# Dynamic filters on one core: Newton step through the PSUM bank of the gelu's input, and all nine products summed by TensorE

## What is computed

```python
h = x
for _ in range(STEPS):                      # STEPS = 5
    t = gelu(einsum('oc,bchw->bohw', W1, h) + b1)
    k = (einsum('oc,bchw->bohw', W2, t) + b2).reshape(B, C, 9, H, W)
    k = k / (norm(k, axis=2) + EPS)         # EPS = 1e-6
    y = sum(patches3x3(h) * k, axis=2)
    h = h + alpha * y
```

## Time and profile before

| | |
|---|---|
| Median of 3 runs | 20135.72 us (20120.86 to 20145.39) |
| Profiled execution | 20080.48 us, span 20078.7 us |
| TensorE / VectorE / ScalarE / GpSimd busy over the span | 62% / 52% / 28% / 47% |
| Mean granted TensorE clock | 0.736 |
| First work of the filter stage | about 15575 us from the start |

### The profile page before, as it was taken

One profiled execution on the slowest core, in us unless ns is written; L12 is line 12 of the kernel. 1 busy time (PEld: TensorE's weight loads), 2 busy tenths in 40 slices (PEclk: granted clock), 3 DMA queues, 4 the chain that ended last, 5 costly groups with the idle time before them and its releaser, 6 DMA issues. The chain is left out here.

```text
span 20078.7 us, 217701 instructions
## 1 busy us (share of the span) xinstructions
PE 12353.6 (62%) x73490; PEld 6114.7 (30%) x73490; DVE 10535.6 (52%) x14652; ACT 5526.4 (28%) x7765; POOL 9453.1 (47%) x8026
## 2 busy tenths in 40 slices
PE   5553699999999202333333333333358899999998
PEld 2551366666666101111111111111112333333332
DVE  4557544444444333443443444344422788888887
ACT  1114333333333000000000000000010666666666
POOL 0113100000000106886887788688800787878787
PEclk9999856656666556666666666666679999999999
DMA  4104222222222494335334433533342112121201
GB/s 94 33 21 102 55 38 36 37 38 36 36 37 38 135 195 111 95 95 131 95 95 107 120 95 95 131 96 95 95 86 58 33 22 42 21 42 22 42 19 30
DMA packets 1399772, 1408.47 MB, mean 70 GB/s; under 512 B 771709, under 2 KB 1116045, under 8 KB 1383565
## 3 DMA queue, kind: packets, MB, share of 16 engines
q1 hardware_dynamic: 1106892, 742.84, 18.5%
q0 software_dynamic: 221184, 604.27, 10.4%
q10 hardware_dynamic: 70976, 50.83, 0.8%
HBM read 1036.74 MB, written 276.84 MB: 65 GB/s over the span
## 5 line engine op out<-in xcount | busy, mean ns | idle before, releaser
L1359 POOL DMA_INDIRECT dc_g<-corners,dc_idx x4608 | 5253.7, 1140 | 1326.0 <-issue 1260.9
L1954 POOL TENSOR_TENSOR df_sq<-df_sq 128x512 f32<-128x512 f32 x1920 | 2713.0, 1427 | 1866.6 <-ACT df_sq L1902 1839.5
L1432 PE MATMUL dc_ps<-ident,dc_s 128*128 128x128 f32 x2560 | 674.0, 428 | 4296.9 <-DVE dc_s L1523 4294.8
L1079 POOL TENSOR_TENSOR nz_vp<-nz_vp,nz_den 128x2048 f32<-128x2048 f32 x16 | 105.8, 6610 | 4814.7 <-DMA nz_den<-den_d 4814.7
L1515 DVE TENSOR_TENSOR dc_g<-dc_g,dc_wt 128x2304 f32<-128x2304 f32 x512 | 1308.6, 2556 | 2001.0 <-DMA dc_g<-corners,dc_idx 2000.9
L1902 ACT ACTIVATE df_sq<-df_pk,vecs 128x512 f32<-128x512 f32 x2880 | 1921.1, 685 | 1326.0 <-DVE df_pr L2056 1309.2
L2056 DVE SCALAR_TENSOR_TENSOR df_pr<-df_pk,vecs,df_h 128x512 f32<-128x512 f32 x2880 | 2047.6, 741 | 407.1 <-PE df_pk L1840 264.5
L1432 PEld LDWEIGHTS dc_ps<-ident,dc_s 128*128 128x128 f32 x2560 | 472.0, 218 | 4480.6 <-DVE dc_s L1523 3352.1
L1392 ACT ACTIVATE dc_st<-dc_ps 128x512 f32<-128x512 f32 x640 | 327.0, 607 | 4934.2 <-PE dc_ps L1432 4934.2
L1840 PE MATMUL df_pk<-df_t,df_wp 64*128 64x512 f32 x3840 | 1389.8, 642 | 364.7 <-ACT df_sq L1902 302.1
L916 DVE TENSOR_REDUCE at_mx<-at_pt 128x4 f32<-128x512 f32 x1024 | 707.8, 691 | 1605.4 <-PE at_pt L779 1605.4
(11 more groups left out here) (271 smaller groups left out, 19428.1 us busy)
## 6 DMA issues: line engine op xcount, KB each, us to landing
df_h<-df_h SPq DMA_DIRECT2D x160, 512.0 KB, 7.1
dc_g<-corners,dc_idx POOLq DMA_INDIRECT x4608, 2.8
corners<-dc_xt SPq DMA_DIRECT2D x16, 4160.0 KB, 41.5
dc_xp<-x SPq DMA_DIRECT2D x8, 4096.0 KB, 40.8
cv_xp<-x SPq DMA_DIRECT2D x8, 4096.0 KB, 50.0
y<-sp_p SPq DMA_DIRECT2D x128, 192.0 KB, 2.8
y<-sp_p SPq DMA_DIRECT2D x64, 384.0 KB, 4.3
at_a<-y SPq DMA_DIRECT2D x64, 384.0 KB
```

Source lines behind the costliest of these rows:

```text
L1359: nc.gpsimd.indirect_dma_start(gt[:, r, k, :, :].rearrange("p a c -> p (a c)"), None, image, bass.IndirectOffsetOnAxis(ap=idx[:, s, r, k:k ...
L1432: i = nc.tensor.transpose(ps[:, j, 128 * r:128 * r + 128], sm[:, r % 2, 128 * j:128 * j + 128], env.ident[:, :])
L1954: nc.gpsimd.tensor_tensor(a, a, sq[:, (KK * n + other) % RING, :], ALU.add).then_inc(nadded, 1)
```

## The change

- GpSimd no longer adds products 6 and 7. TensorE adds products 6, 7 and 8 through the identity, six half-width matmuls in place of two; VectorE's join of y is a copy from PSUM.
- The check writes to the bank `df_p` (p1), which held the gelu's input, instead of to SBUF in place. Refinement reads and writes that bank, and update reads it.
- Check, refinement, update and residual of chunk n - 6 (LAG = 6) stand behind products 0, 1, 2 and 3 of chunk n, in every chunk. The scaling of chunk n - 5 stands behind GpSimd's fourth addition.
- The hidden matmul of chunk n also waits for the update of chunk n - 7; the check waits for the gelu of its own chunk.
- Stores and loads of the raw input go by chunk, with a semaphore for each of four buffers, and the order on SyncE in the last step is new.

```diff
-    BANKS, RING = 5, 15
+    BANKS, RING, LAG = 5, 15, 6
...
+        def wait_update(eng, n):
+            b, step, g = GROUPS[n // CH]
+            if step < STEPS - 1:
+                eng.wait_ge(moved, CH * updates(b, step + 1, g) - CH + n % CH + 1)
+            else:
+                eng.wait_ge(stepout, CH * (b * GR + g) + n % CH + 1)
...
+            def load_raw(o):
+                for src, p in piece(x3, o):
+                    sp.dma_start(rows(ro[p, o % CH, :]), src).then_inc(raw_in[o % CH], 16)
+
+            def store(o):
+                sp.wait_ge(o_out, o + 1)
+                for dst, p in piece(out, o):
+                    sp.dma_start(dst, rows(yo[p, o % CH, :])).then_inc(stored[o % CH], 16)
...
+                for i in range(CH):
+                    o = CH * (b * GR + g) + i
+                    store(o)
+                    if o + CH < CH * B * GR:
+                        load_raw(o + CH)
+                    if i == 1 and g and b + 1 < B:
+                        sp.wait_ge(normed, (b + 1) * GR + g)
+                        copy(g - 1)
+                if b + 1 < B:
                     sp.wait_ge(stepout, CH * (b * GR + g + 1))
-                    if b + 1 < B:
-                        load(b + 1, g)
-                    sp.wait_ge(o_out, CH * (b * GR + g + 1))
...
+                    load(b + 1, g)
...
                 if n:
                     pe.wait_ge(active, n)
+                if n >= LAG + 1:
+                    wait_update(pe, n - LAG - 1)
...
-                for s in range(2):
-                    last = nc.tensor.matmul(py[64 * s:64 * s + 64, :], env.ident[:, 64 * s:64 * s + 64],
-                                            pr[:, (KK * n + 8) % RING, :], start=False, stop=True, tile_position=(0, 64 * s))
+                for k in range(6, KK):
+                    for s in range(2):
+                        last = nc.tensor.matmul(py[64 * s:64 * s + 64, :], env.ident[:, 64 * s:64 * s + 64],
+                                                pr[:, (KK * n + k) % RING, :], start=False, stop=(k == KK - 1), tile_position=(0, 64 * s))
...
-            def singles(n):
-                pool.wait_ge(product, KK * n + 8)
-                a = pr[:, (KK * n + 6) % RING, :]
-                nc.gpsimd.tensor_tensor(a, a, pr[:, (KK * n + 7) % RING, :], ALU.add).then_inc(sadded, 1)
...
                 dve.wait_ge(ysummed, n + 1)
-                dve.wait_ge(sadded, n + 1)
-                nc.vector.tensor_tensor(yr[:, q % 2, c, :], py[:, :], pr[:, (KK * n + 6) % RING, :], ALU.add).then_inc(yjoined, 1)
+                nc.vector.tensor_scalar(yr[:, q % 2, c, :], py[:, :], 1.0, None, ALU.mult).then_inc(yjoined, 1)
...
+            def check(n):
+                q, i = n // CH, n % CH
                 dve.wait_ge(seeded, 2 * q + i // 2 + 1)
-                nc.vector.scalar_tensor_tensor(out=n, in0=n, scalar=env.vecs[:, V_EPS:V_EPS + 1], in1=inv[:, i, :],
+                dve.wait_ge(active, min(n + LAG + 1, NC))
+                if n:
+                    wait_update(dve, n - 1)
+                nc.vector.scalar_tensor_tensor(out=p1[:, :], in0=nr[:, q % 2, i, :], scalar=env.vecs[:, V_EPS:V_EPS + 1], in1=inv[:, i, :],
                                                op0=ALU.add, op1=ALU.mult).then_inc(checked, 1)
...
+            def refine(n):
+                dve.wait_ge(checked, n + 1)
+                dve.wait_ge(scaled, n + 1)
+                nc.vector.scalar_tensor_tensor(out=p1[:, :], in0=p1[:, :], scalar=-2.0, in1=yr[:, n // CH % 2, n % CH, :],
+                                               op0=ALU.add, op1=ALU.mult).then_inc(refined, 1)
...
-            CHECK = {(1, 6): 0, (1, 8): 1, (2, 1): 2, (2, 3): 3}
-            REFINE = {(2, 5): 0, (2, 7): 1, (3, 1): 2, (3, 3): 3}
...
-                    if q >= 2 and c == 0 and k < CH:
-                        update(q - 2, k)
-                    if q >= 2 and c == 0 and 4 <= k < 4 + CH and GROUPS[q - 2][1] == STEPS - 1:
-                        residual(q - 2, k - 4)
+                    if n >= LAG and k < 4:
+                        (check, refine, update, residual)[k](n - LAG)
                     if k == 5 and n:
                         join(n - 1)
-                    if q and (c, k) in CHECK:
-                        check(q - 1, CHECK[c, k])
-                    if q and (c, k) in REFINE:
-                        refine(q - 1, REFINE[c, k])
```

More of the change, by code:

```diff
@@ L1735, in dynamic_filters @@
     copied = [env.sem(f"df_rows_copied{g}") for g in range(GR)]
[L1736 to L1739, removed]
+    w_in, normed, link = (env.sem(n) for n in ("df_w_loaded", "df_normed", "df_chain"))
+    raw_in = [env.sem(f"df_raw_loaded{i}") for i in range(CH)]
+    stored = [env.sem(f"df_stored{i}") for i in range(CH)]
+    hidden, active, tapped, product, squared, nadded = (env.sem(n) for n in (
+        "hidden_done", "gelu_done", "tap_done", "product_done", "square_done", "squares_added"))
     ysummed, nsummed, yjoined, njoined = (env.sem(n) for n in (
@@ L1798, in _ @@
                 copy(g)
+            for o in range(CH):
+                load_raw(o)
             for b, step, g in GROUPS:
-                if step == STEPS - 2 and g == 0:
-                    load_raw(b, 0)
                 if step < STEPS - 1:
@@ L1912, in log @@
                 if q:
+                    act.wait_ge(checked, CH * (q - 1) + 2 * i + 2)
                     act.wait_ge(scaled, CH * (q - 1) + 2 * i + 2)
-                    act.wait_ge(checked, CH * (q - 1) + 2 * i + 2)
                 nc.scalar.activation(inv[:, 2 * i:2 * i + 2, :], nr[:, q % 2, 2 * i:2 * i + 2, :], ACT.Ln,
@@ L2019, in update @@
+            def update(n):
+                b, step, g = GROUPS[n // CH]
                 dve.wait_ge(refined, n + 1)
-                y = rows(yr[:, q % 2, i, :])
                 if step < STEPS - 1:
-                    nc.vector.scalar_tensor_tensor(out=centre(n), in0=y, scalar=alpha[:, 0:1], in1=centre(n), op0=ALU.mult, op1=ALU.add
-                                                   ).then_inc(moved, 1)
+                    nc.vector.scalar_tensor_tensor(out=centre(n), in0=rows(p1[:, :]), scalar=alpha[:, 0:1], in1=centre(n),
+                                                   op0=ALU.mult, op1=ALU.add).then_inc(moved, 1)
@@ L2024, in update @@
                 else:
-                    o = CH * (b * GR + g) + i
+                    o = CH * (b * GR + g) + n % CH
                     if o >= CH:
-                        dve.wait_ge(stored, 32 * (o // CH))
-                    nc.vector.scalar_tensor_tensor(out=rows(yo[:, i, :]), in0=y, scalar=alpha[:, 0:1], in1=centre(n), op0=ALU.mult, op1=ALU.add
-                                                   ).then_inc(stepout, 1)
-            def residual(q, i):
-                b, step, g = GROUPS[q]
-                o = CH * (b * GR + g) + i
-                dve.wait_ge(raw_in, 32 * (o // CH + 1))
-                dve.wait_ge(stepout, o + 1)
-                nc.vector.tensor_tensor(yo[:, i, :], yo[:, i, :], ro[:, i, :], ALU.add).then_inc(o_out, 1)
@@ L2038, in _, with residual @@
-            CHECK = {(1, 6): 0, (1, 8): 1, (2, 1): 2, (2, 3): 3}
-            REFINE = {(2, 5): 0, (2, 7): 1, (3, 1): 2, (3, 3): 3}
+                        dve.wait_ge(stored[o % CH], 32 * (o // CH))
+                    nc.vector.scalar_tensor_tensor(out=rows(yo[:, o % CH, :]), in0=rows(p1[:, :]), scalar=alpha[:, 0:1], in1=centre(n),
+                                                   op0=ALU.mult, op1=ALU.add).then_inc(stepout, 1)
+            def residual(n):
+                b, step, g = GROUPS[n // CH]
+                if step == STEPS - 1:
+                    o = CH * (b * GR + g) + n % CH
+                    dve.wait_ge(raw_in[o % CH], 32 * (o // CH + 1))
+                    dve.wait_ge(stepout, o + 1)
+                    nc.vector.tensor_tensor(yo[:, o % CH, :], yo[:, o % CH, :], ro[:, o % CH, :], ALU.add).then_inc(o_out, 1)
```

64 lines of the change are left out of this document (18 added, 46 removed).

## The result

| | before | after |
|---|---|---|
| Median | 20128.85 us (4 runs, 20120.86 to 20145.39) | 20428.93 us (4 runs, 20424.02 to 20437.20) |
| Profiled execution | 20080.48 us | 20437.20 us |
| Ratio, 95% interval | | 1.0150 (1.0138 to 1.0162) |

The change makes the kernel 300 us slower; 285 was forecast, and 20421 against 20429 in the median.

What follows compares the result with a forecast made beforehand. It took TensorE's order of work, not any full engine, as the bound: stage +276, first chunks +5, drain -18 and clock +22 sum to +285 us, median 20421, 1.4% slower; range 20270 to 20510.

Steps and rivals of the forecast that it cites:

- Floor of a plain chunk: Third and fourth chunks of a group: TensorE's 11.98 us plus 1.72 for two added identity pairs, 13.69.
- First chunk 16.24: Group's first chunk: ScalarE's table load moves from 9.24 to 10.68 us after the sums, so it grows 1.44 to 16.24.
- rival 3: Added matmuls fill TensorE's waits in the groups, so not slower: -70 us, 20066; chance 0.06.
- Second chunk 15.38: Group's second chunk: the 0.80 us wait for the gelu is gone, so it stays at 15.38 us as now.
- Stage +276, clock +22: 79 groups at 59.00 us, 4661 against 4384.7, give +276; the clock's drop meeting the gap differently gives +22.
- Rival 5: Added pairs cost more than 0.86 us, or the lower clock takes two stretches in nearly every group: up to +75; chance 0.08.
- First chunks +5, drain -18: First chunks, without Newton work, add 3 x 1.72 us; the kernel's end shortens by about 18 us.
- Refinement and update at 741 ns: VectorE's refinement (1348 ns) and update (1223 ns), reading one operand from PSUM, take 741 ns each; about 345 us off VectorE.
- New waits cost nothing: The hidden matmul's wait for VectorE's update has 2.6 to 3.7 us of cover; the other new waits also cost nothing.
- Rival 1: TensorE's clock stays at 2.4 GHz through the first chunk's gap: saves 1.69 x 79 = 134 us, 20287; chance 0.17.
- Rival 4: VectorE is the bound, so the 345 us taken off it come off the time: 19791; chance 0.07.

Runs made afterwards that it cites:

- e1: Changed kernel with the old product sum (GpSimd adds products 6 and 7, TensorE sends product 8 alone); 19917.31 us, 0.9897 of the kernel before.
- e3: Changed kernel with two unused matmuls behind tap 3 of each group's second chunk, where TensorE pauses; 20312.65 us, 1.0098 of the kernel before.
- e9: Changed kernel with old product sum, TensorE's sums moved behind tap 3, ScalarE's table work two squares earlier; 0.9813 of the kernel before, 0.9816 when repeated.

## Why the prediction was right

By its own steps, with what was measured:
- *Floor of a plain chunk, 11.98 + 1.72 = 13.69.* Measured 13.66 and 13.69. e1 took 1.71 away again (13.66 to 11.95 in the mean of the third chunk). Right.
- *First chunk 16.24.* Measured 16.21 in the group shown, 16.09 at the least, 16.59 in the mean with the second stretches at the lower clock. The table load was forecast at 10.68 behind the sums and stands at 10.54. That it moves back with tap 7, so that the gap does not swallow the pairs, decided between the forecast and rival 3, and TensorE indeed still waits 2.1 there (1.73 and 0.40), against 2.2 before and 1.9 in the forecast.
- *Second chunk 15.38.* Measured 15.19 here, 15.50 in the mean. The gelu was no longer waited for in this group.
- *Stage +276, clock +22.* Together 298; measured 307. An ordinary group is 58.80, not 59.00 (16 us less over 79), and the short last chunk, which I had set down under the drain, takes 4 more. The term that was too small is the clock: of the 33 groups with a second stretch all but the short last one last 60.1 to 60.8, some 50 us in all where I put 22, a figure for which the prediction gave no working. It was mis-sized by a factor of two, and the rest of the sum hid it: that the total came within 15 us is in part luck. Rival 5's second case, two stretches in nearly every group, came in 33 of 79.
- *First chunks +5, drain -18.* From the first sums to the second group's it is 41.0 us against 35.8, +5.2. The drain is 32.6 against 50.7, -18.1. The forecast had 14 of its 18 for the waits and 4 for the last chunk's length, which lies outside these 18.1: the waits were worth 4 more than I estimated, and the short last chunk was counted there and found in the stage.
- *Refinement and update at 741 ns.* 690 and 742. The check, left at over 741 and up to 1348, takes 767. The sizes did not matter for the time: slack grew to 955 us in front of one instruction.
- *New waits cost nothing.* No wait of the hidden matmul for VectorE is in the trace; around the sums at 17123.70 the update ends 1.35 us after they start and the hidden matmul comes at 6.16, so the cover was 4.8, not 2.6. Right.
- *Rival 1, the clock stays up.* It did not in the changed kernel. Its price of 1.69 a group, 134 us, left out the gelu: by the prediction's own walk tap 0 would then come at 9.8, ahead of the gelu at 10.6, so only 0.8 a group could be won, and e3 shows just that (58.75 to 57.95, with a wait of 0.78). That e3 gave 117 us in all, near 134, is chance: the second stretches in 33 groups, which the rival did not count, made up for it.
- *Rival 4, VectorE is the bound.* Out: it lost 15 points of occupancy while the stage grew. The rule of the Trainium skill, Perfetto Trace Analysis, section Identifying the Most-Contended Engine, taken as the prediction took it (occupancy, and for TensorE the weight loads, without the MFU, the share of peak arithmetic, that the section sets beside them), pointed to VectorE as the engine to relieve. In the old order e1 does bear out that relieving it gains something, 1.0%. As I read the chunks, it gains there because VectorE's operations stood in front of products for which TensorE waits, not because VectorE was full: the fourth chunk, with no such operation, stayed as it was (11.92 and 11.94).

What stays open: why two stretches at the lower clock fall in some groups and one in others was not resolved; only that the pause brings them. How much of the Newton step's worth is its shorter operations and how much its order by chunk was not separated. Another place for ScalarE's tables than that of e9 was not tried, nor were the transfers by chunk run without the new Newton order.

## What to carry to other kernels

Where four engines are 60 to 90% busy, walk one period by the starts of the in-order engine's steps: work added to it in a period that has no wait costs its full length, however idle the engine that it relieves. Before moving work between engines, ask which of its waits it would fill; a wait that begins behind the added work moves back with it and fills nothing. And put work that is ready ahead of the instruction that waits, not behind it: of the two moves in e9 neither gave anything alone on top of e1, both together took 2 us off 53. When a rival or a gain is priced by one wait that goes, look which wait comes to light behind it: in e3 it took back half.

## What was not expected of the hardware

VectorE's check has two inputs in SBUF and the same size in all kernels, yet its mean is 1271 ns before, 767 in the changed kernel, 1253 in e1 and 1465 in e9. The lines, of e1 and of e9:

```profile
L2024 DVE SCALAR_TENSOR_TENSOR df_p<-df_n,vecs,df_inv 128x512 f32<-128x512 f32 x320 | 401.1, 1253 | 1.3 <-ACT df_inv L1942 1.3
```

```profile
L2026 DVE SCALAR_TENSOR_TENSOR df_p<-df_n,vecs,df_inv 128x512 f32<-128x512 f32 x320 | 468.9, 1465 | 1.3 <-ACT df_inv L1944 1.3
```

In all three of the latter it writes to PSUM, so the place of its output does not decide. Nor does it decide how often GpSimd is in the midst of an addition when the check starts: in the changed kernel 312 of 320 checks start so, in e1 316. What differs is how much of that addition is left. One of the kernel before:

```profile
17056.80 1.27 POOL L1959 TENSOR_TENSOR df_pr<-df_pr 128x512 f32<-128x512 f32 x1
17056.96 1.66 DVE L2006 SCALAR_TENSOR_TENSOR df_n<-df_n,vecs,df_inv 128x512 f32<-128x512 f32 x1
```

The addition ends at 17058.07, 1.11 us after the check has started, and the check ends 0.55 later. In the four kernels named above 822 checks start with more than 0.25 us of an addition left, and every one ends 0.55 to 0.56 us after it. Of the other 458, 437 take 0.73 to 0.80. The 21 that are left, 17 of them in e1, meet an addition that starts within 0.06 us of them; they take 1.82 to 1.89 and end 0.55 to 0.56 us after it. Of those that start inside an addition, the mean remainder and the mean duration are 0.18 and 0.76 us in the changed kernel, 0.63 and 1.26 in e1, 0.90 and 1.45 before, 0.91 and 1.47 in e9. So such an operation costs what is left of the addition and 0.56 more, and its place in the order sets the price. This agrees with the Trainium skill, SBUF — State Buffer, section Who interferes with whom: a VectorE instruction with two SBUF inputs contends with a GpSimd instruction that reads SBUF for a port pair that they share, and the hold on it is exclusive. With one input from PSUM, refinement and update take 0.68 to 0.74 us in the mean in every kernel that has them so: 234 of the changed kernel's 320 refinements start inside an addition and take 0.69 like the others. All this is read from the traces of the runs; no run was made for it alone.

Two matmuls of 0.86 us that compute nothing, placed in a pause of 2 us, made the kernel 0.5% faster (1.0098 against 1.0150), by holding the granted clock at 2.4 GHz.
